# Top-2 experts: placing the next block's logits behind the first tile of experts, and the bias split behind the first block's statistics

## The reference

```python
x  = x + h                                   # h: result of the attention stack before
xn = layernorm(x, eps=1e-5)
p  = softmax(xn @ gate_w.T)                  # 8 experts
coef = p where the expert is among the two largest, else 0
y  = sum_e coef[e] * silu(xn @ expert_w[e].T + expert_b[e])
x  = x + y @ combine_w.T
```

## Time and profile before

| | us |
|---|---|
| median of 3 runs | 6759.97 |
| lowest and highest | 6751.65 and 6768.34 |
| the profiled execution, its own time | 6756.28 |
| span of the profiled execution | 6754.2 |
| mean granted clock of TensorE over the span | 0.928 |

### The profile page before, as it was taken

One profiled execution on the slowest core, in us unless ns is written; L12 is line 12 of the kernel. 1 busy time (PEld: TensorE's weight loads), 2 busy tenths in 40 slices (PEclk: granted clock), 3 DMA queues, 4 the chain that ended last, 5 costly groups with the idle time before them and its releaser, 6 DMA issues. The chain is left out here.

```text
span 6754.2 us, 122147 instructions
## 1 busy us (share of the span) xinstructions
PE 5795.9 (86%) x38509; PEld 3594.7 (53%) x38509; DVE 4329.9 (64%) x9722; ACT 2805.1 (42%) x4568; POOL 1939.8 (29%) x2617
## 2 busy tenths in 40 slices
PE   8996999999993998889987998799888889845567
PEld 5773444444442776467745775477545556523454
DVE  6874666666655775367736774477545466669965
ACT  4552222222221554345543554355444455412244
POOL 5440000000003553255414552355310022333312
PEclk9998999999996999899998999899988899867789
DMA  4332222233223553155504551355300000000002
GB/s 129 104 101 91 96 96 95 96 96 97 95 93 82 144 149 94 31 143 146 138 4 131 149 150 33 88 145 149 80 4 0 3 0 0 4 3 0 0 2 57
DMA packets 526309, 526.84 MB, mean 78 GB/s; under 512 B 55698, under 2 KB 436705, under 8 KB 503780
## 3 DMA queue, kind: packets, MB, share of 16 engines
q1 hardware_dynamic: 526004, 523.15, 27.6%
HBM read 337.88 MB, written 185.07 MB: 77 GB/s over the span
## 5 line engine op out<-in xcount | busy, mean ns | idle before, releaser
L362 DVE TENSOR_REDUCE a_mx<-a_unit 128x2 f32<-128x512 f32 (+1 forms) x1920 | 1294.3, 684 | 574.8 <-PE a_unit L538 562.6
L452 ACT ACTIVATE a_prob<-a_slot 128x1536 f32<-128x1536 f32 x640 | 929.0, 1452 | 740.9 <-PE a_slot L561 448.5
L536 PE MATMUL a_unit<-a_sk,a_sq 96*128 96x256 bf16 (+3 forms) x5120 | 756.3, 251 | 75.2 <-DMA a_sk<-a_kscratch 54.1
L1148 ACT ACTIVATE f_silu<-f_pG 128x512 f32<-128x512 f32 x528 | 315.1, 598 | 939.3 <-PE f_pG L1221 939.1
L1094 DVE TENSOR_TENSOR f_gated<-f_spread,f_silu 128x512 f32<-128x512 f32 x512 | 354.3, 692 | 402.8 <-ACT f_silu L1148 358.3
L538 PE MATMUL a_unit<-a_maskq,identb 128*128 128x256 bf16 (+1 forms) x1920 | 606.3, 316 | 0.0
L1200 PE MATMUL f_pO<-f_hidden,f_wd 128*128 128x512 f32 x1056 | 546.3, 599 | 17.0 <-DVE f_hidden L1096 16.3
L536 PEld LDWEIGHTS a_unit<-a_sk,a_sq 96*128 96x128 bf16 (+1 forms) x5120 | 385.3, 99 | 312.1 <-issue 124.8
L1221 PE MATMUL f_pG<-f_xnT,f_wg 128*128 128x512 f32 x1056 | 541.5, 594 | 0.0
L1225 PE MATMUL f_pU<-f_xnT,f_wu 128*128 128x512 f32 x1056 | 540.9, 594 | 0.0
L60 POOL TENSOR_SCALAR f_veps<-f_moments 128x4 f32<-128x4 f32 (+1 forms) x112 | 25.4, 227 | 1731.3 <-DVE f_moments L1002 1271.4
(11 more groups left out here) (394 smaller groups left out, 11507.0 us busy)
## 6 DMA issues: line engine op xcount, KB each, us to landing
f_spread<-f_scratch SPq DMA_DIRECT2D x1024, 128.0 KB, 2.9
a_sq<-a_qscratch SPq DMA_DIRECT2D x128, 768.0 KB, 5.7
a_sk<-a_kscratch SPq DMA_DIRECT2D x160, 384.0 KB, 6.6
a_qscratch<-a_parts SPq DMA_DIRECT2D x288, 192.0 KB, 2.2
a_qscratch<-a_parts SPq DMA_DIRECT2D x288, 128.0 KB, 2.2
a_kscratch<-a_parts SPq DMA_DIRECT2D x160, 192.0 KB, 2.2
a_kscratch<-a_parts SPq DMA_DIRECT2D x160, 128.0 KB, 2.1
a_qscratch<-a_parts SPq DMA_DIRECT2D x288, 64.0 KB, 1.8
```

The costliest lines, as they stand in the source:

```text
L362: v.tensor_reduce(dst, src, op=ALU.max, axis=AX.X, negate=True).then_inc(red_done, 1)
L452: act.activation(prob[gr % 2][:, :], slot[:, :], ACT.Exp, scale=SCALE).then_inc(exp_done, 1)
L536: pe.matmul(bank[:, at * wide:(at + 1) * wide], q, sk[b][0:KM, gr * GH + h, 0:wide], start=(at == 0), stop=False)
L1148: act.activation(silu[c % 2][:, :], pG[c % 2][:, :], ACT.Silu).then_inc(silu_done, 1)
```

## The change

Two parts move; nothing is added or removed, and no transfer changes.

- On TensorE the block of logits of block n+1, with its two waits, leaves the head of the step and goes behind the whole of tile 0 (its `turn_mixed`, `experts` and `combine`), ahead of tile 1.
- On VectorE the seven instructions that split the bias become a function `split_bias`, called in step -2 behind `ln_apply` of block 0, and the wait for `w_in` goes with them. On TensorE the wait for `bias_done` goes from the head of the program to the first `experts`.

```diff
@block.vector
-                v.wait_ge(w_in, W_IN)
...
-                chain.link(v.tensor_copy(bpart[:, 0, :], be[:, :]))
...
+                def split_bias():
+                    v.wait_ge(w_in, W_IN)
+                    chain.link(v.tensor_copy(bpart[:, 0, :], be[:, :]))
...
                         ln_apply(v, rows(core["x"], (n + 2) * BT, BT), moments, rstd, xn).then_inc(xn_done, 1)
+                    if once(n, -2):
+                        split_bias()
                     if within(n + 1):
                         probable(n + 1)
@block.tensor
-                pe.wait_ge(bias_done, 1)
                 ident = core["ident"]
 
                 def experts(n, b, t):
+                    if once(n, 0) and t == 0:
+                        pe.wait_ge(bias_done, 1)
...
                 def step(n, b):
-                    if within(n + 1):
-                        pe.wait_ge(xnT_done, n + 2)
-                        if later(n, 0):
-                            pe.wait_ge(max_done, n + 1)
-                        for t in range(BT):
-                            ins = pe.matmul(pL[:, t * E:(t + 1) * E], xnT[1 - b][:, t * P:(t + 1) * P], wgate[:, :],
-                                            start=True, stop=True)
-                        ins.then_inc(logit_pe, 1)
                     for t in range(BT):
                         back = within(n) if t >= LAG else later(n, 1)
+                        if t == 1 and within(n + 1):
+                            pe.wait_ge(xnT_done, n + 2)
+                            if later(n, 0):
+                                pe.wait_ge(max_done, n + 1)
+                            for u in range(BT):
+                                ins = pe.matmul(pL[:, u * E:(u + 1) * E], xnT[1 - b][:, u * P:(u + 1) * P], wgate[:, :],
+                                                start=True, stop=True)
+                            ins.then_inc(logit_pe, 1)
                         if back:
                             turn_mixed(n * BT + t - LAG, t - LAG)
```

More of the change, by code:

```diff
@@ L1294, in _ @@
                 chain = Chain(v)
-                v.wait_ge(w_in, W_IN)
                 def tt(out, a, b, op):
                     chain.link(v.tensor_tensor(out, a, b, op=op))
-                chain.link(v.tensor_copy(bpart[:, 0, :], be[:, :]))
[L1301 to L1308, removed]
+                def split_bias():
+                    v.wait_ge(w_in, W_IN)
+                    chain.link(v.tensor_copy(bpart[:, 0, :], be[:, :]))
+                    tt(brest[:, :], be[:, :], bpart[:, 0, :], ALU.subtract)
+                    chain.link(v.tensor_copy(bpart[:, 1, :], brest[:, :]))
+                    tt(bpart[:, 2, :], brest[:, :], bpart[:, 1, :], ALU.subtract)
+                    chain.link(v.tensor_scalar(bpick[:, :], bpart[:, 0, :], core["ident"][0:3, 0:1], None, ALU.mult))
+                    chain.link(v.scalar_tensor_tensor(out=brest[:, :], in0=bpart[:, 1, :], scalar=core["ident"][0:3, 1:2],
+                                                      in1=bpick[:, :], op0=ALU.mult, op1=ALU.add))
+                    v.scalar_tensor_tensor(out=b3[:, :], in0=bpart[:, 2, :], scalar=core["ident"][0:3, 2:3],
+                                           in1=brest[:, :], op0=ALU.mult, op1=ALU.add).then_inc(bias_done, 1)
                 def statistics(m):
```

## The result

The changed kernel takes 6669.03 us (median of 4 runs, 6666.31 to 6672.29) against 6755.81 us for the kernel before on the same chip (6746.72 to 6768.34): ratio 0.987, 95% interval 0.9853 to 0.9888. The forecast was 6674 us, range 6658 to 6722. The profiled execution took 6666.91 us, 89.4 us less than the one before.

The account below looks back on a forecast made before the run. TensorE sets the pace, slowed by stops for ScalarE's copy `xnT` and the low clock behind them. 74.2 + 7.8 + 4.5 = 86.5 us off 6756.28, plus 3.7 for the median, gives 6674 us, range 6658 to 6722.

Parts of the forecast that it names:

- Term A: Silu(1, 0) to Silu(15, 0): with the logits behind tile 0, 321.03 us become 246.8, 74.2 us saved.
- the clock comes back: TensorE in the changed stage: without the stops the low clock that follows each goes too, 45.7 of 74.2 us saved.
- The rival by which it is the kind of work in the step that makes the clock fall: TensorE's low clock comes from how it works here, not from the stop, and stays: 6721 us, 18% chance.
- The rule of the Trainium skill: Cycling through PSUM buffers, micro-idles between groups of matmuls make TensorE's clock swing; by it the time is near 6721 us.
- Term B: Start of the stage: block 0's normalising goes under the DMA wait for the weights; its experts begin 7.8 us earlier.
- Term C: Silu(0, 0) to Silu(1, 0): 23.72 us become 19.2, 4.5 us saved if the clock has risen, otherwise only 1 us.
- The end of the stage: The last step and the stage's end, with the other stages, stay as they are.
- Covers: VectorE reaches the logits 4.63 us after Silu(n, 0), at least 2.3 us of cover; ScalarE's copy is about 2 us early.
- the rivals that put a new wait in the old one's place: Another engine becomes the bound, 6707 us, 6%; ScalarE's copy is later too, 6752 us, 2%; logits too late for routing, 1%.

Follow-up runs that it names:

- bare wait: Changed kernel with TensorE's wait for `xnT` moved back to the head of the step, the logits still behind tile 0: 6750.54 us, ratio to before 0.9984.
- the fill: Kernel before plus nine unneeded identity matmuls at the head of each step, ahead of the wait for `xnT`: 6711.12 us, ratio 0.9923.
- part 2 by itself: Changed kernel with the logits back at the head of TensorE's step, so only the bias split is moved: 6753.98 us, ratio to before 0.9992.
- part 1 by itself: Changed kernel with the bias split back at the front, so only the logits are moved behind tile 0: 6681.74 us, ratio to before 0.9878.
- the late split: Changed kernel with the bias split one step later still, behind the normalising of block 1: 6675.22 us, ratio to before 0.9878.
- the shortened stop: Kernel before with ScalarE making the copy `xnT` ahead of SiLU of tile 3, TensorE's order untouched: 6695.85 us, ratio 0.9907.
- the kernel without the bias: Changed kernel without the 128 bias matmuls, so the experts' bias is left out of the result: 6623.19 us, ratio to before 0.9803.
- the fill at the start of the stage: Kernel with the bias split behind block 1, plus 14 and 22 unneeded identity matmuls ahead of TensorE's waits for weights and bias: 6662.51 us, ratio to before 0.9863.

## Why the prediction was right

**Term A, Silu(1, 0) to Silu(15, 0).** 246.8 us were forecast and 246.77 are in the trace (5042.02 to 5288.79), so 74.3 us saved for 74.2. The step of 17.66 us, put together from one tile at the end of the stage, three tiles in its middle and one group of logits, is what the stage does in each of its blocks. It could be read off because the stage before held stretches at either clock, and the sum took only rows at the full one.

**Why the clock comes back.** This carried over half the gain, and was the step with the weakest ground. It is now shown from three sides: a bare wait at the same place lowers the clock with nothing else changed; matmuls that nothing needs, in place of the idle time, keep it up though `xnT` comes as late; a stop of 0.6 us in place of 2.2 keeps it up, but for one fall in 14, with the logits where they were. What stays open is the single stop: the clock fell behind 10 of 14 bare waits of 2.2 to 2.5 us. The rival by which it is the kind of work in the step that makes the clock fall expected 6700 us with the bare wait and 6756 us with the fill; 6750.5 and 6711.1 were measured. The rule of the Trainium skill ("TensorE: Matmul & The Clock Gate", section "A second HAM failure mode: psum-queue depth-cycling") that I had set against the forecast is not borne out in the changed kernel: the stage cycles through its two `pE` buffers for 258 us at 1.00. TensorE has no idle time in that stretch, however, so this shows that cycling alone does not lower the clock; it does not try the short idles of which the rule speaks. For those there are the stops of some 0.6 us above, with one fall in 14.

**Term B, the bias split.** 7.8 us forecast. Against the stage's start, Silu(0, 0) comes at 32.50 us before and 24.75 after: 7.75 us. The experts began at 5017.80 where 5018.4 was forecast, and those 0.6 us are the earlier start of the whole stage. The term needs both parts: part 2 by itself brings Silu(0, 0) 4.9 us forward (27.59 us from the stage's start), part 1 by itself 2.3 us (30.23), as the logits of block 1 no longer stand ahead of block 0's experts.

**Term C, block 0 to block 1.** 19.2 us forecast, 19.04 measured (5022.98 to 5042.02); the clock had risen in time, from 5032 us on. The prediction named this as a condition and had no ground for it: with the late split the clock rose after 5 us of experts, here after 15, so that it held is in part luck, worth 3.5 us at most by the prediction's own sum.

**The end of the stage.** Forecast as unchanged: 21.29 us from Silu(15, 0) to the next stage's first DMA issue in both traces. The three terms and this one make 74.3 + 7.75 + 4.7 + 0 = 86.7 us, the whole of the stage's gain. The 5 us by which the median undercut the forecast are no term of the sum: the comparison has a fourth run of the kernel before, of 6746.72 us, and with it the median that the forecast started from is 6755.81 us and not 6759.97, 4.2 us lower.

**Covers.** VectorE comes for the logits 4.65 us behind Silu(n, 0) (4.63 forecast), with 3.8 us to spare; the copy is 1.8 us early (2 forecast). Neither of the rivals that put a new wait in the old one's place took place.

## What to carry to other kernels

Look at what stands first in the in-order list of the engine that sets the pace: if it is work for a later block that hangs on the last instruction of another engine, move it behind work whose inputs are long there, and check that the engine that reads its result comes later still (here 3.8 us). If TensorE's granted clock is below 1.00 in a stage where it is otherwise busy, price each stop as the stop plus the slow stretch behind it; here 2.2 us of stop cost 5.3 us a step. A fill that keeps TensorE busy shows in one run how much of a loss is clock, and a bare wait shows it from the other side.

## What the runs showed of the hardware

- Stops of 2.2 to 2.5 us, once in some 22 us of dense work, brought the mean granted clock of a stage to 0.84 and 0.87; stops of 0.6 us at the same place left it at 0.99. The single stop can go either way: with the bare wait, no low clock followed four of the 14 stops; with the shortened stop, one followed one of 14; a stop of 0.54 us in each step of the kernel without the bias left the clock at 1.00 from 5040 to 5240 us; and a single stop of 2.09 us lowered the clock in one kernel and not in another. What decides in the single case was not tried.
- At the start of dense work the low clock lasted 15 us in the changed kernel (5017 to 5032 us, 0.50) and 5 us with the late split (5009.5 to 5014.3 us, 0.52).
- I had not expected the fill at the start of the stage to be given back: the wait for block 2's rows stayed as long (2.09 us), but the clock fell behind it, which cost 3.2 us.
- A bf16 matmul of 3 rows and 512 columns ahead of each f32 matmul costs 0.51 us of TensorE's time here (a tile with two of them takes 4.09 us, one without 3.06), more than the 0.31 us from its start to the start of the next matmul.
